# Writing the zeros of the slots' buffer from the first stage on, and pairing the scatters of two mixtures with the shared expert's units

## The chip, the cores and the metric

One Trainium2 chip, one core. The metric is the time of one execution in microseconds of the device, the median of several runs. Engines: PE is TensorE (PEld its weight loads), DVE is VectorE, ACT is ScalarE, POOL is GpSimd, SP is SyncE, which here only issues DMAs; a q behind a name is that engine's sequencer.

## The reference

Sixteen sequences of 128 tokens with 256 features go through four layers. Each layer adds `tanh(g) * attention(layernorm(x))` and then `tanh(g) * ffn(layernorm(x))`. The attentions differ (a decaying sum of the context, masked attention, 32 small heads, attention over channels). The ffn of layer 0 is one linear map. Those of layers 1 to 3 are mixtures of 16 experts beside a shared expert:

```python
logits = h @ router_w.T                       # layer 1; layers 2 and 3 have routers of their own
top_vals, top_idx = jax.lax.top_k(softmax(logits), K)        # K = 4, 2, 4 in layers 1, 2, 3
y = einsum('eni,eih->enh', silu(g) * u, w_down)              # each expert: gate, up, down
routed = einsum('enh,ne->nh', y, comb)
shared = silu(h @ sh_gate) * (h @ sh_up) @ sh_down           # the shared expert, on every token
```

## The kernel before

All tokens stay on the chip as 16 blocks of 128 (`x`, normed in `xn_wide` with 8 more columns of marks). The program is a chain of stages, each a `nc.Block()` in which every engine has its own list of instructions: `setup_and_decay` (attention of layer 0), `linear` (ffn of layer 0), `masked_attention` (layer 1), `mixture(1)`, `many_heads` (attention of layer 2), `mixture(2)`, `channel_heads`, `mixture(3)`, `combine_last`. At the end of a block all five engines meet at a barrier; some stages are followed by a second one (L2566, L2549), where semaphores are freed. A DMA that is in flight needn't have landed at a barrier, but the instruction that issues it has to be over.

A mixture works in two parts. In the first, TensorE, ScalarE and VectorE run the shared expert over all tokens in units: for each pair of blocks, `pieces` units (6 in layer 1, so 48 units; 2 in layer 2, so 16 units). A unit is gate and up products (L2147, or L2152 for the narrow last unit of a pair), the gate activation on ScalarE (L2306, semaphore `sh_gated`, one step a unit), the product with up on VectorE (L2432) and the down product (L2166). In layer 1 the pairs 3 to 6 are a loop at run time. Beside it VectorE routes the tokens: it gives each token a slot row for each of its experts (`row_in`; semaphore `placed`). In layer 1 it does so in two groups of 8 blocks.

GpSimd then scatters the tokens to their slots in DRAM: one indirect DMA per block and choice, 128 rows of 1056 bytes, into `slots_in`. In layer 1 these are 16 x 4 = 64 scatters, all in the mixture. In layer 2 they are 32, of which 14 go out in the attention stage and 18 in the mixture, from block 7 on (L2053). In layer 3 36 go out in the attention stage and the rest in the mixture.

In the second part of a mixture the experts' tiles are worked: SP loads tile by tile from `slots_in` (L2076, only when all scatters have landed), TensorE turns it and multiplies, and GpSimd scatters the results to `slots_out` (L2059).

Not every slot of `slots_in` gets a token, so the whole buffer is filled with zeros first. `write_zeros` (L191 to L194) issues on SP's queue one DMA of 2112 KB for each of the 16 experts, whose source is the cleared tile `xs_wide`. Before the change 5 of them are issued in `linear`, 5 in `masked_attention` and 6 in `mixture(1)`. GpSimd waits for all 16 (`zeroed`) before the first scatter of mixture 1.

`masked_attention` also prepares the gate biases of layer 2: SP loads `bias_raw`; GpSimd splits it in three bf16 parts (L571 to L574) and clears `gbias` (L575); SP writes the parts to DRAM (L559) and reads them back as rows (L562). At L2589 (`root`) GpSimd takes roots of variances for the next norm; `root(pool, 8)` and `root(pool, 9)` end its part of `masked_attention`.

Of the kernel before, what the change touches and what calls it, by code (L numbers as in the profile page):

```python
# [27 lines left out]
NE = 16  # L28
# [99 lines left out]
def _build(nc, io, top):  # L128
# [52 lines left out]
    ZEROS = NE  # L181
# [8 lines left out]
    def write_zeros(eng, first, end):  # L190
        of_block = slots_in.rearrange("(t p) d -> p t d", p=P)  # L191
        for e in range(first, end):
            eng.dma_start(of_block[:, e * NB:(e + 1) * NB, :], xs_wide[:, 0:1, :].broadcast_to([P, NB, W])
                          ).then_inc(zeroed, 16)  # L194
# [49 lines left out]
    def setup_and_decay(measure, root, stats_ready, rooted, zeroed):  # L244

        with ExitStack() as st:
# [1 line left out]
            x_in = [sem(f"x_in{i}") for i in range(4)]  # L248
            ctx_in = [sem(f"ctx_in{i}") for i in range(4)]
            (cleared, gates_ready, own, cw_ready, based, beta_added, sums_done, sumT_ready, in_done, inT_ready,  # L250
             s_done, s_copied, spread, summed, g_ready, x_ready, w_ready) = (
                sem(n) for n in ("cleared", "gates", "own", "cw", "based", "beta", "sums", "sumT", "in", "inT",
                                 "s", "sc", "spread", "summed", "g", "x", "w"))
            numbers_i = sb("numbers_i", [P, ROUTED], I32, st)
            lanes_i = sb("lanes_i", [P, 4], I32, st)
            base_i = sb("base_i", [P, NE], I32, st)
# [16 lines left out]
            @block.sync  # L273
            def _(sp):
                for i in range(4):
                    sp.dma_start(x[:, quarter(i)], io["x"][:, quarter(i)]).then_inc(x_in[i], 16)
                for i in range(4):
                    sp.dma_start(ctx[:, quarter(i)], io["ctx"][:, quarter(i)]).then_inc(ctx_in[i], 16)
                sp.dma_start(ctxT[:], io["ctxT"]).then_inc(ctxT_loaded, 16)
                load_experts(sp, 1)  # L280

            @block.scalar
            def _(act):
# [15 lines left out]
            @block.gpsimd  # L299
            def _(pool):  # L300
                nc.gpsimd.memset(ident[:], 0.0).then_inc(cleared, 1)
                nc.gpsimd.memset(ones[:], 1.0).then_inc(cleared, 1)
                nc.gpsimd.memset(neg_half[:], -0.5).then_inc(cleared, 1)
                pool.iota(numbers_i[:], pattern=[[1, ROUTED]], base=0, channel_multiplier=0).then_inc(cleared, 1)
                pool.iota(lanes_i[:], pattern=[[0, 4]], base=1, channel_multiplier=1).then_inc(cleared, 1)
                pool.iota(base_i[:], pattern=[[NB * P, NE]], base=1, channel_multiplier=0).then_inc(cleared, 1)
                pool.iota(token_i[:], pattern=[[4 * P, NB], [1, 4]], base=-int(FAR), channel_multiplier=4
                          ).then_inc(cleared, 1)
                pool.iota(spare_i[:], pattern=[[P, 8]], base=4 * NB * P - int(FAR), channel_multiplier=1
                          ).then_inc(cleared, 1)  # L310
                pool.wait_ge(cleared, 8)
                nc.gpsimd.affine_select(out=ident[:], in_=ident[:], compare_op=ALU.not_equal, fill=1.0, base=0,
                                        pattern=[[-1, P]], channel_multiplier=1).then_inc(cleared, 1)
                nc.gpsimd.memset(xs_wide[:], 0.0)
                nc.gpsimd.tensor_copy(numbers[:], numbers_i[:])
                for i in range(4):
                    nc.gpsimd.tensor_scalar(lanes[:, i:i + 1], lanes_i[:, i:i + 1], TAG * i, None, ALU.add)
                nc.gpsimd.tensor_copy(expert_base[:], base_i[:])
                nc.gpsimd.tensor_copy(token_rows[:], token_i[:])
                nc.gpsimd.tensor_copy(spare_rows[:], spare_i[:])  # L320
                root(pool, 0)
                root(pool, 1)
                pool.wait_ge(own, 9)
                for b in range(NB):
                    pool.wait_ge(based, b + 1)
                    nc.gpsimd.tensor_tensor(x[:, b, :], x[:, b, :], gg[:, 1, :], ALU.add).then_inc(beta_added, 1)
                pool.wait_ge(w_ready, 1)
                for c in range(C):
                    nc.gpsimd.tensor_tensor(w[:, c, :], w[:, c, :], small["l0_scale"], ALU.mult)
                for b in range(NB):  # L330
                    pool.wait_ge(stats_ready, NB + b + 1)
                    nc.gpsimd.tensor_tensor(xn[:, b, :], xn[:, b, :], gg[:, 0, :], ALU.mult).then_inc(g_ready, 1)
                    if b == 8:
                        root(pool, 2)
                for i in (3, 4, 5):
                    root(pool, i)
# [111 lines left out]
    def linear(measure, root, stats_ready, rooted, kept, blocked):  # L448

        with ExitStack() as st:  # L450
# [3 lines left out]
            block = st.enter_context(nc.Block())  # L454
            XT, Y = bank[0:2], bank[2:6]

            @block.sync
            def _(sp):
                write_zeros(sp, 0, 5)

            @block.gpsimd
            def _(pool):
                for b in range(NB):
# [68 lines left out]
    def masked_attention(measure, root, stats_ready, rooted, kept, blocked):  # L532
        carve = carver(1)
        with ExitStack() as st:
# [16 lines left out]
            def there(b):  # L551
                return 0 <= b < NB

            @block.sync
            def _(sp):
                sp.dma_start(bias_raw, io["l2_gub"]).then_inc(b_in, 16)
                for i in range(3):
                    sp.wait_ge(b_parted, i + 1)
                    sp.dma_start(bias_rows[i].rearrange("(p j) -> p j", j=NE * 2), bias_part[i]).then_inc(b_out, 16)  # L559
                sp.wait_ge(b_out, 48)  # L560
                sp.wait_ge(b_parted, 7)
                sp.dma_start(gbias[0:3], bias_rows).then_inc(b_back, 16)  # L562
                write_zeros(sp, 5, 10)
                sp.wait_ge(b_back, 16)

            @block.gpsimd
            def _(pool):
                step = Chain(pool, b_own)
                pool.wait_ge(b_in, 16)
                for i in range(3):  # L570
                    nc.gpsimd.tensor_copy(bias_part[i], bias_raw).then_inc(b_parted, 1)  # L571
                    if i < 2:
                        pool.wait_ge(b_parted, i + 1)
                        step(nc.gpsimd.tensor_tensor(bias_raw, bias_raw, bias_part[i], ALU.subtract))  # L574
                nc.gpsimd.memset(gbias[:], 0.0).then_inc(b_parted, 1)  # L575
                nc.gpsimd.memset(three_ones[:], 0.0).then_inc(b_parted, 1)
                pool.wait_ge(b_parted, 5)
                nc.gpsimd.memset(three_ones[0:3], 1.0).then_inc(b_parted, 1)
                pool.wait_ge(b_parted, 6)
                pool.sem_inc(b_parted, 1)  # L580
                root(pool, 8)
                root(pool, 9)

            @block.tensor
            def _(pe):
# [1350 lines left out]
    def mixture(layer, rt, carve, t0, scattered, late=0):  # L1936
# [11 lines left out]
        with ExitStack() as st:  # L1948
# [44 lines left out]
            of_group = lambda g, at: bank[3][:, at:at + NE * (groups[g][1] - groups[g][0])]  # L1993
            PRE = [of_group(g, 0).rearrange("p (t e) -> p t e", e=NE) for g in range(len(groups))]
            CNT = [of_group(g, D).rearrange("p (e t) -> p e t", e=NE) for g in range(len(groups))]
            ahead = NB // 2
            late_xT = row_space[:, 7 * D:8 * D].rearrange("p (c q) -> p c q", c=C)
            front_x = lambda b: xT[:, b % 2] if b < ahead else late_xT
# [41 lines left out]
            @block.gpsimd  # L2040
            def _(pool):
                if layer < 3:
                    make_before(pool, rt, tri_ready)
                if layer == 1:
                    nc.gpsimd.tensor_copy(xn_wide[:, :, D + 4:D + 8], token_rows[:]).then_inc(marked, 1)
                    pool.wait_ge(marked, 1)
                if layer == 1:
                    pool.wait_ge(zeroed, 16 * ZEROS)
                for t in range(t0 - late // k, NB):
                    if t in [g[0] for g in groups]:  # L2050
                        pool.wait_ge(placed, 2 * [g[0] for g in groups].index(t) + 2)
                    for i in range(k):
                        pool.indirect_dma_start(out=slots_in, in_=xn_wide[:, t, :], in_offset=None,  # L2053
                                                out_offset=bass.IndirectOffsetOnAxis(ap=row_in[:, t, i:i + 1], axis=0)
                                                ).then_inc(scattered, 16)
                for n in range(total):
                    pool.wait_ge(y_copied, n + 3)
                    pool.wait_ge(places, n + 1)
                    pool.indirect_dma_start(out=slots_out, in_=y[:, n % U, :], in_offset=None,  # L2059
                                            out_offset=bass.IndirectOffsetOnAxis(ap=y_rows[:, n % U:n % U + 1], axis=0)  # L2060
                                            ).then_inc(stored[n % U], 16)

            @block.sync
            def _(sp):
                if layer == 1:
                    write_zeros(sp, 10, ZEROS)
                held = sp.alloc_register(f"block{layer}")
                blocks = slots_in.rearrange("(b p) d -> p b d", p=P)

# [606 lines left out]
```

## Time and profile before

| | us |
|---|---|
| median of 3 runs | 1409.24 |
| lowest, highest | 1405.26, 1410.93 |
| profiled execution, its time | 1406.2 |
| its span, first to last instruction | 1404.5 |
| TensorE busy (matmul) | 1105.6, 79% |
| VectorE busy | 753.7, 54% |
| GpSimd busy | 609.9, 43% |
| ScalarE busy | 487.8, 35% |

Times in the rows are microseconds from the span's start. A row of a timeline gives start, duration, engine, line of the kernel, operation, what is written and read, the number of instructions merged in the row, and in square brackets how long the engine stood idle before it and what released it; "issue" means that it waited for nothing that the profile shows. Lines are those of the kernel before. Issue instructions of DMAs on SP are shown with the time that SP spent on them, which isn't the time to landing.

### The profile page before, as it was taken

The numbers are of one execution on the slowest core, as the hardware profiler recorded it, in microseconds if no ns is written. First come the engines' busy times: TensorE is split into PE (matmuls) and PEld (weight loads), VectorE is DVE, ScalarE is ACT, GpSimd is POOL, SyncE is SP. The second block draws the span as 40 slices with busy tenths as digits, with TensorE's granted clock in tenths as the row PEclk, the third lists the DMA queues.
The fourth block names the chain that finished last, engine by engine and source line by source line (L and its number), as shares of the span: only waits on it lengthen the run. The fifth ranks groups of instructions, "written<-read, shape, count | busy, mean of one in ns | idle before, by whom it ended". The sixth has DMA issues, their size and how long they took to land. (4 is left out here: it accounts for less than half of the span.)

```text
span 1404.5 us, 25581 instructions
## 1 busy us (share of the span) xinstructions
PE 1105.6 (79%) x7222; PEld 815.2 (58%) x7223; DVE 753.7 (54%) x2787; ACT 487.8 (35%) x1309; POOL 609.9 (43%) x961
## 2 busy tenths in 40 slices
PE   4476984399999996799997779958887756599980
PEld 4364863287777774466665567845554434478770
DVE  6857432013444444687862555557777554365557
ACT  0054210011333332266653124424764422144440
POOL 5552056600333334565552404545564554345560
PEclk9998896699999998699996999977998876899995
DMA  9598942200333333211500114540002311256547
GB/s 407 160 309 266 340 142 89 92 0 16 104 106 106 106 106 107 77 47 61 219 25 32 66 43 134 155 157 2 2 2 117 137 67 66 85 136 165 145 132 299
DMA packets 92302, 169.45 MB, mean 121 GB/s; under 512 B 11103, under 2 KB 70751, under 8 KB 91231
## 3 DMA queue, kind: packets, MB, share of 16 engines
q1 hardware_dynamic: 72825, 114.71, 26.2%
q0 software_dynamic: 17664, 48.91, 9.6%
q10 hardware_dynamic: 1728, 4.79, 0.9%
q8 instruction: 44, 0.72, 0.2%
q14 instruction: 41, 0.33, 0.1%
HBM read 82.75 MB, written 85.61 MB: 120 GB/s over the span
## 5 line engine op out<-in xcount | busy, mean ns | idle before, releaser
L2236 PE MATMUL bank<-weights,xT 128*128 x832 | 241.0, 412 | 0.8 <-ACT xT L2330 0.7
L2059 POOL DMA_INDIRECT slots_out<-weights,y_rows x128 | 123.2, 962 | 155.3 <-DVE y_rows L2501 81.8
L2059 POOL DMA_INDIRECT slots_out<-pack,y_rows x80 | 77.0, 962 | 199.4 <-DVE y_rows L2501 190.8
L2053 POOL DMA_INDIRECT slots_in<-xn_wide,row_in x110 | 106.4, 968 | 124.1 <-DMA slots_in<-xs_wide 50.2
L2236 PEld LDWEIGHTS bank<-weights,xT 128*128 128x128 f32 x832 | 142.4, 191 | 25.9 <-issue 2.2
L2147 PE MATMUL bank<-xT,weights 128*128 128x256 f32 x416 | 113.0, 420 | 20.3 <-ACT xT L2294 16.7
L2330 ACT COPY xT<-bank 128x256 f32<-128x256 f32 x208 | 77.5, 373 | 111.3 <-PE bank L2228 104.2
L1471 PE MATMUL bank<-ctx,weights 32*128 32x256 f32 x512 | 80.5, 461 | 37.5 <-DVE weights L1627 27.9
L2147 PEld LDWEIGHTS bank<-xT,weights 128*128 128x128 f32 x416 | 85.7, 211 | 40.1 <-ACT xT L2294 14.1
L2432 DVE TENSOR_TENSOR rows<-rows,bank 128x256 f32<-128x256 f32 (+1 forms) x56 | 22.5, 402 | 147.4 <-ACT rows L2306 105.7
L1544 ACT ACTIVATE weights<-bank 128x512 f32<-128x512 f32 x128 | 72.6, 597 | 79.0 <-PE bank L1479 60.7
L1627 DVE TENSOR_REDUCE weights<-bank 128x2 f32<-128x512 f32 x128 | 86.0, 682 | 21.1 <-PE bank L1471 16.2
L2166 PE MATMUL bank<-weights,rows 128*128 128x256 f32 x256 | 73.4, 404 | 28.1 <-issue 21.8
L2478 DVE TENSOR_TENSOR weights<-weights,bank 128x128 f32<-128x128 f32 x128 | 36.9, 288 | 92.8 <-ACT weights L2334 83.9
L2306 ACT ACTIVATE rows<-bank 128x256 f32<-128x256 f32 (+1 forms) x56 | 20.7, 370 | 185.7 <-PE bank L2147 97.1
L1471 PEld LDWEIGHTS bank<-ctx,weights 32*128 32x128 f32 x512 | 51.5, 216 | 54.2 <-issue 24.4
L2253 PE MATMUL bank<-weights,pack 88*128 x320 | 82.2, 379 | 0.0
L1479 PE MATMUL bank<-weights 32*128 32x256 f32 x512 | 78.9, 451 | 1.4 <-ACT weights L1544 1.4
L2253 PE MATMUL bank<-weights 128*128 x256 | 77.3, 385 | 0.8 <-ACT weights L2338 0.8
L2478 DVE TENSOR_TENSOR pack<-pack,bank 128x176 f32<-128x176 f32 x80 | 27.1, 338 | 92.5 <-ACT pack L2334 78.7
L971 ACT ACTIVATE weights<-bank 128x512 f32<-128x512 f32 x128 | 71.5, 605 | 12.2 <-PE bank L865 11.8
L2166 PEld LDWEIGHTS bank<-weights,rows 128*128 128x128 f32 x256 | 48.7, 201 | 42.4 <-issue 33.3
(432 smaller groups left out, 2479.7 us busy)
## 6 DMA issues: line engine op xcount, KB each, us to landing
slots_in<-xs_wide SPq DMA_DIRECT2D x16, 2112.0 KB, 18.9
weights<-slots_in SPq DMA_DIRECT2D x96, 132.0 KB
xs_wide<-slots_in SPq DMA_DIRECT2D x72, 132.0 KB
weights<-slots_out SPq DMA_DIRECT2D x17, 512.0 KB, 17.4
rows<-slots_out SPq DMA_DIRECT2D x16, 512.0 KB, 3.3
weights<-in_l_gu SPq DMA_DIRECT2D x1, 7040.0 KB
pack<-slots_in SPq DMA_DIRECT2D x40, 132.0 KB
weights<-in_l_gu SPq DMA_DIRECT2D x1, 4608.0 KB, 16.2
```

The costliest lines, as they stand in the source:

```text
L971: nc.scalar.activation(e[:, G * c + g].rearrange("p j q -> p (j q)"), S[g][:], ACT.Exp, scale=HD ** -0.5).then_inc(e_ready, 1)
L1471: last = nc.tensor.matmul(score_bank(N * bs + ns)[:, j * L:(j + 1) * L], xh[bs % 2][rows, j, qh * P:(qh + 1) * P], ctx[rows, bs, :], start ...
L1479: last = nc.tensor.matmul(key_bank(N * b + n)[:, j * L:(j + 1) * L], km[b % 2][rows, j, c * P:(c + 1) * P], xm[b % 2][rows, j, :], start=T ...
L1544: nc.scalar.activation(eT[:, n].rearrange("p j q -> p (j q)"), key_bank(t)[:], ACT.Exp, scale=HD ** -0.5).then_inc(e_ready, 1)
L1627: nc.vector.tensor_reduce(peak[b % 2][:, qh, at:at + step_j + 1:step_j], score_bank(s)[:].rearrange("p (j l) -> p j l", j=2), AX.X, ALU.ma ...
L2053: pool.indirect_dma_start(out=slots_in, in_=xn_wide[:, t, :], in_offset=None, out_offset=bass.IndirectOffsetOnAxis(ap=row_in[:, t, i:i + 1 ...
L2059: pool.indirect_dma_start(out=slots_out, in_=y[:, n % U, :], in_offset=None, out_offset=bass.IndirectOffsetOnAxis(ap=y_rows[:, n % U:n % U ...
L2147: last = nc.tensor.matmul(out[:, side * D:(side + 1) * D], shared_gu[:, c, at:at + P], xp[:, c, :], start=(c == 0), stop=(c == C - 1))
L2166: last = nc.tensor.matmul(s_Y[t % 2][:, 0:D], sh_h4[:, n % ring, u * P:(u + 1) * P], shared_dn[:, i, :], start=(i == 0), stop=(i == pieces ...
L2236: last = nc.tensor.matmul(out, xT[:, n.c % 2, c, :], flat(gu_w[:, ds(e, 1), c, :]), start=(c == 0), stop=(c == C - 1 and layer != 2))
L2253: last = nc.tensor.matmul(Y[n.c % 2][:, 0:D], hT[:, n.c % 2, i, :], flat(dn_w[:, ds(e, 1), i, :]), start=(i == 0), stop=(i == parts - 1))
L2330: nc.scalar.copy(flat(xT[:, n.c % 2]), XT[n.c % 2][:, 0:D]).then_inc(xT_ready, 1)
```

## The change

- `write_zeros` for all 16 experts stands at the end of SP's list in `setup_and_decay`, behind all loads and behind a new semaphore `blank`, which GpSimd raises when it has cleared `xs_wide`. The calls in `linear`, `masked_attention` and `mixture(1)` go.
- The four small DMAs for the gate biases in `masked_attention` are issued by GpSimd instead of SP, in the same order. GpSimd waits for the three stores before `root(pool, 8)`, and for the read back at its end.
- In mixtures 1 and 2 GpSimd waits before every second scatter for one more `sh_gated`: pair m for gate 10 + m in layer 1 (gates 10 to 41 of 48), for 6 + m in layer 2 (6 to 14 of 16). Layer 3 is unchanged.

```diff
             @block.sync                      # setup_and_decay
                 load_experts(sp, 1)
+                sp.wait_ge(blank, 1)
+                write_zeros(sp, 0, ZEROS)
...
-                nc.gpsimd.memset(xs_wide[:], 0.0)
+                nc.gpsimd.memset(xs_wide[:], 0.0).then_inc(blank, 1)
...
-            @block.sync                      # linear
-            def _(sp):
-                write_zeros(sp, 0, 5)
...
-            @block.sync                      # masked_attention
-            def _(sp):
-                sp.dma_start(bias_raw, io["l2_gub"]).then_inc(b_in, 16)
-                for i in range(3):
-                    sp.wait_ge(b_parted, i + 1)
-                    sp.dma_start(bias_rows[i].rearrange("(p j) -> p j", j=NE * 2), bias_part[i]).then_inc(b_out, 16)
-                sp.wait_ge(b_out, 48)
-                sp.wait_ge(b_parted, 7)
-                sp.dma_start(gbias[0:3], bias_rows).then_inc(b_back, 16)
-                write_zeros(sp, 5, 10)
-                sp.wait_ge(b_back, 16)
             @block.gpsimd
                 step = Chain(pool, b_own)
+                pool.dma_start(bias_raw, io["l2_gub"]).then_inc(b_in, 16)
                 pool.wait_ge(b_in, 16)
...
-                pool.sem_inc(b_parted, 1)
+                for i in range(3):
+                    pool.dma_start(bias_rows[i].rearrange("(p j) -> p j", j=NE * 2), bias_part[i]).then_inc(b_out, 16)
+                pool.wait_ge(b_out, 48)
+                pool.dma_start(gbias[0:3], bias_rows).then_inc(b_back, 16)
                 root(pool, 8)
                 root(pool, 9)
+                pool.wait_ge(b_back, 16)
...
+            send_from = {1: 10, 2: 6, 3: 0}[layer]          # mixture
...
                     for i in range(k):
+                        if layer < 3 and i % 2 == 0:
+                            pool.wait_ge(sh_gated, send_from + ((t - t0) * k + i) // 2)
                         pool.indirect_dma_start(out=slots_in, in_=xn_wide[:, t, :], in_offset=None,
...
             @block.sync                      # mixture
-                if layer == 1:
-                    write_zeros(sp, 10, ZEROS)
```

## Rows read from the trace of the kernel before

**Rows 1.** List of waits, whole span: who for whom, us in total, times, longest

```profile
POOL slots_in L2053 <- DMA slots_in<-xs_wide: 50.2, 1, 50.2
```

**Rows 2.** Timeline of GpSimd: attention stage, mixture 1, tiles of mixture 2

```profile
119.61 1.64 POOL L2589 TENSOR_TENSOR rstd<-var,neg_half 128x8 f32<-128x8 f32 x1 [7.66 <-DVE var L2583]
...
132.28 0.20 POOL L2591 TENSOR_TENSOR offset<-nmean,rstd 128x8 f32<-128x8 f32 x1
136.35 0.21 POOL L1931 MEMSET pack<- 128x128 f32 x1 [3.87 <-POOLq L2566]
...
187.38 1.24 POOL L2053 DMA_INDIRECT slots_in<-xn_wide,row_in  x1 [50.23 <-DMA slots_in<-xs_wide]
...
226.93 0.96 POOL L2053 DMA_INDIRECT slots_in<-xn_wide,row_in  x1 [0.30 <-issue]
234.19 0.96 POOL L2053 DMA_INDIRECT slots_in<-xn_wide,row_in  x1 [6.30 <-DVE xn_wide L1869]
...
273.56 0.96 POOL L2053 DMA_INDIRECT slots_in<-xn_wide,row_in  x1 [0.31 <-issue]
...
902.03 0.96 POOL L2059 DMA_INDIRECT slots_out<-weights,y_rows  x1 [0.77 <-issue]
```

**Rows 3.** Timeline of TensorE in mixture 1: first and last of each slow stretch

```profile
202.40 0.44 PE L2152 MATMUL bank<-xT,weights 128*64 128x128 f32 x4
...
230.74 0.59 PE L2166 MATMUL bank<-weights,rows 128*128 128x256 f32 x1 [1.51 <-issue]
...
252.07 0.27 PE L2152 MATMUL bank<-xT,weights 128*64 128x128 f32 x1 [0.45 <-issue]
...
278.06 0.59 PE L2166 MATMUL bank<-weights,rows 128*128 128x256 f32 x1 [2.21 <-issue]
```

**Rows 4.** Timeline of ScalarE in mixture 1: gates of units 12, 30 and 48

```profile
187.99 0.28 ACT L2306 ACTIVATE rows<-bank 128x128 f32<-128x128 f32 x1
...
298.46 0.28 ACT L2306 ACTIVATE rows<-bank 128x128 f32<-128x128 f32 x1
...
344.46 0.28 ACT L2306 ACTIVATE rows<-bank 128x128 f32<-128x128 f32 x1 [1.51 <-PE bank L2152]
```

**Rows 5.** Timeline of TensorE in mixture 2

```profile
811.40 3.78 PE L2147 MATMUL bank<-rows,weights 128*128 128x256 f32 x8 [7.93 <-ACT rows L2294]
```

**Rows 6.** DMAs of zeros: ns to issue (min/median/max), and us to landing

```profile
L193 SPq DMA_DIRECT2D slots_in<-xs_wide x16: 389/6212/6849, 72.1 to 166.6; - x16
...
DMA to landing us min/median/max: 7.9/18.9/19.9
```

**Rows 7.** The page's DMA issues: count, KB each, median us to landing

```profile
slots_in<-xs_wide SPq DMA_DIRECT2D x16, 2112.0 KB, 18.9
```

**Rows 8.** Timeline of SP: the last loads' issue, and the zeros' issues merged

```profile
9.49 1.38 SPq L215 DMA_DIRECT2D weights<-in_l_sdn  x1
72.07 21.73 SPq L193 DMA_DIRECT2D slots_in<-xs_wide  x5
...
112.37 60.77 SPq L193 DMA_DIRECT2D slots_in<-xs_wide  x11
```

**Rows 9.** Waits of SP's queue at barriers after stage one, linear, attention (two)

```profile
SPq L246 <- PEq L246: 61.0, 1, 61.0
...
SPq L450 <- PEq L450: 3.5, 1, 3.5
...
SPq L2566 <- PEq L2566: 0.7, 1, 0.7
...
SPq L534 <- PEq L534: 0.2, 1, 0.2
```

**Rows 10.** Windows: length, busy of PE, PEld, DVE, ACT, POOL, clock, DMA share, GB/s

```profile
50.00:60.00 10.00, 1.82 (x5) 0.91 (x3) 9.90 (x28) 0.00 (x0) 8.33 (x11) 1.00 0.69 159
...
62.00:64.00 2.00, 0.00 (x0) 0.00 (x0) 1.90 (x11) 0.00 (x0) 0.51 (x1) 1.00 0.26 104
...
140.00:173.00 33.00, 31.02 (x168) 27.25 (x167) 15.09 (x76) 8.97 (x23) 0.00 (x0) 0.80 1.09 340
```

**Rows 11.** The page's DMA queues: packets, MB, share of 16 engines

```profile
q8 instruction: 44, 0.72, 0.2%
```

More of the change, by code:

```diff
@@ L250, in setup_and_decay @@
             (cleared, gates_ready, own, cw_ready, based, beta_added, sums_done, sumT_ready, in_done, inT_ready,
-             s_done, s_copied, spread, summed, g_ready, x_ready, w_ready) = (
+             s_done, s_copied, spread, summed, g_ready, x_ready, w_ready, blank) = (
                 sem(n) for n in ("cleared", "gates", "own", "cw", "based", "beta", "sums", "sumT", "in", "inT",
-                                 "s", "sc", "spread", "summed", "g", "x", "w"))
+                                 "s", "sc", "spread", "summed", "g", "x", "w", "blank"))
             numbers_i = sb("numbers_i", [P, ROUTED], I32, st)
```

## The prediction

> **What bounds the kernel now.** I read the list of waits first, then the timelines of SP, GpSimd, TensorE and ScalarE in the first 345 us, and last the DMA windows. The waits point to GpSimd: its first scatter of mixture 1 stands 50.2 us waiting for the zeros [rows 1]. That wait by itself costs little. Mixture 1 begins at 136.35 [rows 2], TensorE and ScalarE work on the shared expert meanwhile, and nothing there needs the scatters yet. The price comes after. Scatters run back to back from 187.38 to 227.9 and from 234.19 to 274.5, one every 1.27 us (0.96 busy, 0.30 between) [rows 2]. From 202.40 TensorE starts single matmuls "issue"-idle between them until 230.74, and again from 252.07 until 278.06 [rows 3]. It waits for no engine's data there; it is slow in starting its own instructions. Both times it comes back 3 to 5 us after the last scatter of the run.
>
> Size of that stall: the gate activations of the shared expert stand at 298.46 and at 344.46 with 18 units between, so an undisturbed unit takes 46.0 / 18 = 2.56 us. From 187.99 (12th gate) to 344.46 (48th) there are 36 units: 92 us undisturbed, 156.5 us in the trace [rows 4]. **64 us are lost to the scatters.** In mixture 2 one stall of the same look costs 7.9 us [rows 5].
>
> The other thing to see is SP. Its issue of a 2112 KB DMA of zeros takes 6.2 us in the median and 0.4 at the least, and such a DMA lands up to 19.9 us after its issue [rows 6, 7]: SP gets about two of them ahead of the DMA engines, then stands until one has landed. Five hold it 21.7 us, eleven 60.8 us [rows 8]. And the end of each stage is a barrier that SP joins. At the end of the attention stage SP waited 0.2 us at the first barrier (L534) and 0.7 at the second (L2566) [rows 9], so it came last; GpSimd was done at 132.48 and began again at 136.35 after 3.87 us idle [rows 2]. The five zeros of that stage held up all engines for 3.87 - 0.9 - 0.2, say 2.8 us.
>
> **The change, part by part.**
>
> *Zeros from stage one.* All 16 now stand behind the loads on SP's queue, in a stage that ends at 72 us and in which SP today waits 61.0 us for the others at the barrier [rows 9]. SP has issued its loads at 10.9 us [rows 8]. The DMA engines are busy with the loads to about 64 us: share 0.69 in 50 to 60, still 0.26 in 62 to 64 [rows 10]. Some engines are done earlier, but each DMA of zeros is spread over them, and its landing waits for the slowest. Zeros move at 340 GB/s with the engines full (share 1.09) [rows 10]: 2112 KB is 2.163 MB, 6.35 us each, 16 make 101.6 us. If the slowest engine starts at 62, the last lands at 163; if all work had been packed evenly, at about 156. Today the last issue ends at 112.37 + 60.77 = 173.1 and the zeros are there at 187.4 at the latest, 14 us later [rows 2, 8]. So SP leaves stage one at 163 - 13 = 150; bounds 143 and 156. The other engines are done at 72.0 and stand. **Cost +78 us** (+71 to +84). Nothing hides it: no work of another stage can pass the barrier.
>
> *What this takes away.* The 2.8 us at the end of the attention stage go. In the linear stage SP reached its barrier 3.5 us early [rows 9], so the five zeros that leave it were covered: 0. The eleven later issues lay beside mixture 1's work: 0.
>
> *Bias rows by GpSimd.* Four small DMAs move from SP's queue to GpSimd's. GpSimd idles 7.66 us before its root at 119.61 [rows 2], and the zeros have landed before this stage begins, so transfers meet empty engines. Four issues at the 0.96 us of its scatters are 4 us, plus landings of a few us. Only the last root (ready at 132.48) is on the path. Cost 0; upper bound 8 us, should each of the three waits take 5 us and only the idle time absorb them; below nothing it can't go, since SP did the same in a hidden place.
>
> *Scatters of mixture 1 in pairs.* Before each pair GpSimd waits for one more gate, from the 10th to the 41st. Queued behind this wait are only more scatters; who waits for them is SP (all 64) before it loads tiles. The 41st gate is 7 units or 18 us before the 48th, so the loads aren't late. The 64 scatters start where they start today, at the 10th gate instead of 187.38 in today's time, and need 32 units instead of two runs of 41 us.
>
> Does this keep TensorE going? A pair costs GpSimd 2 x (0.96 + 0.30) = 2.52 us, and an undisturbed unit is 2.56 us. So the pairs leave almost no pause; the rate is that of today's runs. What the wait does give is feedback: if TensorE stalls, no gate comes, the scatters stop after the present pair, and TensorE recovers after 3 to 5 us. Today's stalls begin 15 and 18 us after a run begins [rows 2, 3]. 32 units are 82 us, so about five stalls, each 4.4 us (recovery, with part of the pair before it): 22 us come back. **Gain 64 - 22 = 42 us.** Bounds: 64, if pairs never stall it (in mixture 2's tiles one scatter every 1.7 us goes on without such idle time [rows 2]); and about 5, if every loop turn and every instruction block of each engine stalls 6 to 8 us. I take the middle, for the density is nearest to that of today's runs.
>
> The Trainium skill ("Runtime: NRT & Kernel Launch", Instruction fetch mechanics) says that each engine's instructions come in 16 KiB blocks over a DMA queue of its own, and that a taken branch can force such a fetch. The page's instruction queue shows 44 packets and 0.72 MB, 16 KB each [rows 11], which agrees. By that rule stalls would fall where an engine needs its next block while scatters are going, more often in the loop of pairs 3 to 6, and the gain would be nearer 30 than 64.
>
> *Scatters of mixture 2.* 18 in nine pairs, behind gates 6 to 14 of 16. Today's stall is 7.9 us [rows 5]; one short one may remain: **gain 4 us** (0 to 8). The last pair leaves two units, some 5 us, for landing and loads, which just do.
>
> **Sum.** +78 - 2.8 - 42 - 4 = +29 us on the profiled execution (1406.2 us, span 1404.5): 1435 us. The median of the runs shown, 1409.24, is 3 us above it; I say **1437 us**.
>
> **Rivals.**
> 1. *Held at stage one, stalls partly back* (above): 1420 to 1462. Chance 0.50.
> 2. *Held, but pairs remove all stalls.* +78 - 2.8 - 64 - 8 = +3: about 1412, 1404 to 1420. For it: steady scatters in the tiles disturb nobody. Against: 2.52 of 2.56 us is no pause. Chance 0.26. With it the kernel is unchanged as measured.
> 3. *SP isn't held in stage one*, because the queue takes more DMAs than seen or zeros overtake the tail of the loads. Then SP leaves below 72 us and the sum is -2.8 - 42 - 4 = -49, about 1360, down to 1335 with all stalls gone. It decides from the point where SP's last issue ends before 72 us. Against it: the loads do go out without a hold, in 10.9 us, but the third DMA of zeros already waits for the first one to land [rows 6, 7, 8]. Chance 0.09.
> 4. *Pairs don't help*: every unit with scatters is slow. With a gain of 5 in all the sum is +70: 1480. For it: same density and now twice as many units under scatters. Against it: the feedback. Chance 0.15.
>
> Beside rival 3, the Trainium skill ("DMA: Bandwidth & Descriptors", Issuing engines are not separate DMA queues) says that DMAs of all issuing engines share the same 16 engines and that issuing costs the sequencer little. By this rule SP would be away early and the time would be rival 3's; the trace's 6.2 us issue is against it.
>
> **How the numbers follow.** 0.5% is 7 us, about what a measurement can tell from no change. Faster (below 1402): rival 3 and a sliver of 2, 0.11. Same (to 1416): most of rival 2 and little of 1, 0.19. Slower: the rest, 0.70. Range: 1404 to 1472, which leaves out rival 3 and half of rival 4, about 0.2; the likeliest case's own is 1420 to 1462.
>
> **What the new profile would show.** SP's zeros follow its loads without a gap, its last issue ends near 150; all other engines idle from 72 to about 150, released by the barrier; the linear stage starts there. If it starts at 72, rival 3 holds. The attention stage lasts 36 us instead of 38.8. In mixture 1 scatters stand in pairs behind ScalarE's gates, the 12th to 48th gate take about 114 us (92: rival 2; above 145: rival 4), and TensorE's "issue" idle falls into short pieces of 3 to 5 us. Mixture 2's shared expert is 4 us shorter. Everything behind is shifted and otherwise as before. The prediction is wrong first of all if the hold in stage one is not 71 to 84 us; next if the pairs' stalls are not about a third of today's.

## The result and the profile after

The changed kernel takes 1433.59 us (median of 4, 1429.44 to 1437.66), the kernel before in the same comparison 1410.09 (4, 1405.26 to 1414.42): ratio 1.0167, 95% interval 1.0123 to 1.0212. It is slower by 1.7%. The forecast was 1437 us, and "slower" had a chance of 0.70. The profiled execution took 1429.44 us with a span of 1427.6, 23.1 more than before.

The timeline of SP in the changed kernel (start, duration; 16 issues in one row), and its list of waits from 60 to 220 us:

```profile
11.09 142.02 SPq L193 DMA_DIRECT2D slots_in<-xs_wide  x16
```

```profile
ACT xn_wide L495 <- PEq L246: 115.6, 1, 115.6
...
DVE kept L512 <- PEq L246: 83.4, 1, 83.4
```

SP stands in its issues from 11.09 to 153.1, and the others stand at the barrier of stage one (L246). The windows show how completely (columns: busy us of PE, PEld, DVE, ACT and POOL with instructions, granted clock, DMA share, GB/s):

```profile
0.00:72.00 72.00, 33.15 (x112) 27.02 (x113) 51.68 (x158) 2.95 (x7) 39.27 (x68) 1.00 0.93 326
72.00:153.00 81.00, 0.00 (x0) 0.00 (x0) 0.00 (x0) 0.00 (x0) 0.19 (x1) 1.00 1.08 342
```

For 81 us no engine works and the DMA engines write zeros at 342 GB/s, the rate of [rows 10]. ScalarE began the linear stage at 72.08 before and begins it at 153.53 now, 81.5 us later.

The timeline of GpSimd, changed kernel: the bias rows' read back, the start of mixture 1, its first and last scatter. They answer to [rows 2]:

```profile
189.79 0.57 POOL L570 DMA_DIRECT2D gbias<-bias_rows  x1 [1.42 <-DMA bias_rows<-pack]
...
214.36 0.21 POOL L1922 MEMSET pack<- 128x128 f32 x1 [1.54 <-POOLq L2558]
...
262.77 1.13 POOL L2047 DMA_INDIRECT slots_in<-xn_wide,row_in  x1 [47.62 <-ACT rows L2298]
...
359.76 0.96 POOL L2047 DMA_INDIRECT slots_in<-xn_wide,row_in  x1 [0.30 <-issue]
```

Mixture 1 starts 78.0 us later than before (136.35). By the first rows of ScalarE in each stage the attention stage takes 36.2 us instead of 38.8, so it gave back 2.6, and the linear stage 24.6 instead of 25.5. GpSimd waits for a gate now, not for zeros. The gates of units 12 and 48, timeline of ScalarE, against [rows 4]:

```profile
266.80 0.28 ACT L2298 ACTIVATE rows<-bank 128x128 f32<-128x128 f32 x1
...
381.14 0.28 ACT L2298 ACTIVATE rows<-bank 128x128 f32<-128x128 f32 x1 [1.51 <-PE bank L2144]
```

114.3 us instead of 156.5: 42 came back. But the stalls that remain look different from those of before. From the timeline of the changed kernel, all engines, 281 to 288 us:

```profile
281.61 0.38 ACT L2298 ACTIVATE rows<-bank 128x256 f32<-128x256 f32 x1 [2.21 <-PE bank L2139]
...
282.37 1.09 PE L2144 MATMUL bank<-xT,weights 128*64 128x128 f32 x16
...
284.00 0.96 POOL L2047 DMA_INDIRECT slots_in<-xn_wide,row_in  x1 [0.30 <-issue]
286.68 0.59 ACT L2286 COPY xT<-bank 128x512 f32<-128x512 f32 x1 [4.68 <-remote]
...
287.72 0.96 POOL L2047 DMA_INDIRECT slots_in<-xn_wide,row_in  x1 [2.75 <-ACT rows L2298]
```

The products of the narrow unit are over at 283.46, TensorE goes on without a pause, and ScalarE's copy, which waits for them, starts 3.2 us later, with no releaser of this kernel ("remote"). Then TensorE and GpSimd both wait for ScalarE. This comes about once in each pair of blocks. From 262 to 385 us the matmuls have only 1.0 us of "issue" idle left.

The shift over time: 81.5 at the start of the linear stage, 78.0 at the start of mixture 1, 36.7 at its end, 35.8 at the first pair of mixture 2, 26.5 at the start of `channel_heads`, 23.1 at the end.

### The profile page after: what moved, and what is told of

Read it like the earlier page. It is cut to its first block and busy times, and to the rows that moved or that the text cites. A ratio compares the mean times of both kernels' runs of the same rounds, so it can differ in the third digit from the quotient of the medians.

```text
span 1427.6 us, 25582 instructions
## 1 busy us (share of the span) xinstructions
PE 1093.3 (77%) x7222; PEld 807.5 (57%) x7223; DVE 754.1 (53%) x2787; ACT 487.8 (34%) x1309; POOL 613.1 (43%) x966
## 5 line engine op out<-in xcount | busy, mean ns | idle before, releaser
L2139 PEld LDWEIGHTS bank<-xT,weights 128*128 128x128 f32 x416 | 86.2, 213 | 45.2 <-issue 23.6
L1618 DVE TENSOR_REDUCE weights<-bank 128x2 f32<-128x512 f32 x128 | 86.0, 682 | 19.5 <-PE bank L1462 16.1
L477 PE MATMUL bank<-ident,xn_wide 128*128 128x128 f32 x32 | 6.7, 300 | 102.2 <-ACT xn_wide L495 102.2
L2158 PE MATMUL bank<-weights,rows 128*128 128x256 f32 x256 | 69.6, 394 | 7.6 <-DVE x L2432 6.2
```

What stands on the lines that cost most here:

```text
L1618: nc.vector.tensor_reduce(peak[b % 2][:, qh, at:at + step_j + 1:step_j], score_bank(s)[:].rearrange("p (j l) -> p j l", j=2), AX.X, ALU.ma ...
L2139: last = nc.tensor.matmul(out[:, side * D:(side + 1) * D], shared_gu[:, c, at:at + P], xp[:, c, :], start=(c == 0), stop=(c == C - 1))
L2158: last = nc.tensor.matmul(s_Y[t % 2][:, 0:D], sh_h4[:, n % ring, u * P:(u + 1) * P], shared_dn[:, i, :], start=(i == 0), stop=(i == pieces ...
```

## Experiments: the two halves apart

Theory: the zeros cost about 80 us because SP is held at the barrier of stage one, and the pairs gain some 50 by themselves. Rival: the halves are tied together (fewer zeros in flight make the stall smaller, not the pairs). Four kernels, on one chip, on which the kernel before took 1406.10. Whether the 1433.59 of the changed kernel come from the same chip isn't known.

**Pairs alone** is the kernel before plus

```diff
+            send_from = {1: 10, 2: 6, 3: 0}[layer]
...
+                        if layer < 3 and i % 2 == 0:
+                            pool.wait_ge(sh_gated, send_from + ((t - t0) * k + i) // 2)
```

> The kernel before with the waits of the pairs alone; zeros and bias rows stay where they were. Theory (the two halves of the change add up): the linear stage starts at 72, the 12th to the 48th gate take about 114 us as in the changed kernel instead of 156, mixture 2's gates are 13 us shorter and its tiles lose 3: 1410 - 42 - 13 + 3 = 1358 us (1350 to 1370). The scatters still start at 187.4, when the last zeros are there. Rival (the stalls became smaller because the zeros had left the DMA engines, not because of the pairs): 12th to 48th gate stay above 145 us, and the time is 1395 to 1410.

Measured: 1355.01 us (1347.03 to 1361.49), ratio 0.9609 (0.953 to 0.9688). 12th to 48th gate 110.1 us.

**Zeros alone** is the changed kernel without those waits.

> The changed kernel without the waits of the pairs: all 16 DMAs of zeros from stage one, bias rows by GpSimd, scatters back to back. Theory: linear stage starts at 153, 81 us late, 3 come back at the end of the attention stage, and the scatters cost TensorE the same 64 us as before: 1410 + 81 - 3 = 1488 us (1480 to 1495). Rival (the zeros were part of that stall): 12th to 48th gate come down to about 114 us without pairs, and the time is about 1433 to 1446.

Measured: 1484.33 us (1482.24 to 1489.85), ratio 1.0541 (1.0468 to 1.0613); 12th to 48th gate 150.4 us. Both expected times held, and the halves add up: the pairs are worth 51.1 us without the zeros' move (1406.1 - 1355.0) and 50.7 with it (1484.3 - 1433.6), nearer to each other than the spread of the runs (8 to 14 us) can tell. The rival falls.

This kernel also shows what comes late. TensorE, VectorE and ScalarE in the timeline of zeros alone, while 32 scatters run from 260.06 to 300.31:

```profile
285.41 0.73 PE L2137 MATMUL bank<-xT,weights 128*128 128x256 f32 x1 [1.03 <-issue]
306.24 0.77 PE L2172 MATMUL bank<-pack 128*128 128x128 f32 x2 [20.11 <-issue]
```

```profile
305.86 0.22 DVE L1812 TENSOR_SCALAR pack<-pack 128x128 f32<-128x128 f32 x1
```

```profile
291.72 0.38 ACT L2296 ACTIVATE rows<-bank 128x256 f32<-128x256 f32 x1 [18.10 <-issue]
305.11 0.66 ACT L2296 ACTIVATE rows<-bank 128x256 f32<-128x256 f32 x2 [13.01 <-remote]
```

The product that the gate of 291.72 takes was over at 277.27 by TensorE's rows, and those of the two gates at 305.11 by 286.2. TensorE's own 20.11 us are a consequence, though the row says "issue": in the kernel its next instruction (L2172) waits for VectorE's choice of experts (L1812), and VectorE's list has that behind its product with the gate of 305.11. What TensorE loses directly is smaller: single matmuls that start 0.8 and 1.03 us late, like those of [rows 3], in the middle of a unit, where the kernel has no wait. ScalarE comes back 4.8 us after the last scatter of the run.

The kernel before has the same. The timeline of its ScalarE:

```profile
218.82 0.38 ACT L2306 ACTIVATE rows<-bank 128x256 f32<-128x256 f32 x1 [19.46 <-remote]
232.90 0.38 ACT L2306 ACTIVATE rows<-bank 128x256 f32<-128x256 f32 x1 [13.70 <-remote]
```

By the rows the product for the first of them was over at 199.02. But the trace also records the updates of semaphores, which these views don't list: TensorE's update for this product stands at 218.80, 19.8 us after that, and ScalarE starts 0.02 us after the update. In the changed kernel the copy of 286.68 has its update at 286.60, for products over at 283.46. ScalarE's and VectorE's own updates come at once in the same place (199.37 for a gate that ends at 199.36, 199.82 for a product that ends at 199.81). So ScalarE isn't slow to start: **late is TensorE's signal to it, or the true end of TensorE's product**, since the ends of matmuls are modelled. "remote" says just this, that an update came with no instruction ending beside it. The first late one in the kernel before is that of the gate of 198.97, whose product was over at 195.77, 8 us after the first scatter.

**Eight zeros first**: only the count in stage one changes, the other 8 go out in mixture 1.

```diff
-                write_zeros(sp, 0, ZEROS)
+                write_zeros(sp, 0, 8)
...
+                if layer == 1:
+                    write_zeros(sp, 8, ZEROS)
```

> The changed kernel, but only 8 DMAs of zeros from stage one and 8 from mixture 1. Theory: what holds SP is the count of DMAs, 6.24 us each: it leaves stage one at 153.1 - 8 x 6.24 = 103.2, 31 us late. The eight in mixture 1 take 50 us and land by about 180, before the 10th gate. 1434 - 50 = 1384 us (1377 to 1392). Rival (SP waits for the landing of the loads, or for all of its DMAs at the barrier): stage one ends above 115 and the time is above 1396.

Measured: 1378.64 us (1368.06 to 1383.91), ratio 0.977 (0.9686 to 0.9853). ScalarE begins the linear stage at 102.73: 30.7 us late, 31 were expected. So the cost follows the count: 8 DMAs more cost 81.5 - 30.7 = 50.8 us, 6.35 each, the time in which the DMA engines move one.

**Zeros dealt out**, 3, 4, 5 and 4 by stage:

```diff
-                write_zeros(sp, 0, ZEROS)
+                write_zeros(sp, 0, 3)
...
+            @block.sync
+            def _(sp):
+                write_zeros(sp, 3, 7)
...
+            @block.sync
+            def _(sp):
+                write_zeros(sp, 7, 12)
...
+                if layer == 1:
+                    write_zeros(sp, 12, ZEROS)
```

> Pairs and bias rows by GpSimd as in the changed kernel, with the zeros dealt out so that they fit into each stage: 3 from stage one (the third issue ends at 153.1 - 13 x 6.24 = 72.0), 4 in the linear stage (25 us of 25), 5 in the attention stage (31 of 36) and 4 in mixture 1. Theory: no stage ends late, the attention stage is 3 us shorter, scatters begin with the 10th gate: 1434 - 81 = 1353 us (1346 to 1360), below the kernel with pairs alone by 3 to 6 us. Rival: the third issue of stage one or the fourth of the linear stage ends late by one DMA, and each such miss gives 6 us back: 1358 to 1366.

Measured: 1349.48 us (1335.0 to 1351.62), ratio 0.9545 (0.9459 to 0.9632). The linear stage starts at 72.56 (72.20 with pairs alone) and mixture 1 at 134.39 (136.48): no stage is held, 2 us are gained there. The difference to pairs alone, 5.5 us, is within the spread of the two.

## Experiments: what is it in the scatters

My theory was feedback: at the density of before, starving (matmuls and signals of TensorE that come late for no cause in the program) begins after some 15 us, and the wait for a gate lets the engines recover. The rivals were the density itself, the loop, and the bytes. Four kernels with one profiled execution each, on a second chip, on which the kernel before took 1409.62.

**Paced**: the kernel before, no waits on gates, but a small piece of work between two scatters of mixture 1.

```diff
+    pace_space = sb("pace_space", [P, 128])
...
+                        if layer == 1:
+                            nc.gpsimd.memset(pace_space[:], 0.0).then_inc(paced, 1)
+                            pool.wait_ge(paced, t * k + i + 1)
```

> The kernel before with no waits on gates: GpSimd only clears 128x128 elements after each scatter of mixture 1 and waits for that, which makes one scatter every 1.6 us or so instead of 1.27. In the changed kernel the 64 stand 1.54 us apart on average (262.77 to 359.76). Theory (feedback: the scatters must stop when a gate is late): pacing alone doesn't stop the starving, 12th to 48th gate stay above 135 us (before 156.5). Rival (rate: density alone decides): 12th to 48th gate come to 105 to 120 us as with the pairs.

Measured: 1345.54 us, 12th to 48th gate 96.8 us. The timeline of GpSimd in it, and the windows (columns as above):

```profile
200.05 0.96 POOL L2055 DMA_INDIRECT slots_in<-xn_wide,row_in  x1 [0.28 <-issue]
201.02 0.22 POOL L2059 MEMSET pace_space<- 128x128 f32 x1
201.51 0.96 POOL L2055 DMA_INDIRECT slots_in<-xn_wide,row_in  x1 [0.28 <-issue]
```

```profile
200.00:227.00 27.00, 25.79 (x141) 21.09 (x140) 9.95 (x40) 5.61 (x14) 21.93 (x37) 1.00 0.26 95
```

One scatter every 1.46 us instead of 1.27, for all of the 92 us, and TensorE is busy 25.8 of 27 us; in the same stretch of before it was 8.4, at a clock of 0.64 instead of 1.00. The same stretch of before:

```profile
200.00:227.00 27.00, 8.43 (x30) 4.72 (x29) 2.98 (x16) 0.38 (x1) 20.29 (x23) 0.64 0.29 105
```

Nothing stopped the scatters when an engine was late, so feedback isn't needed: **my theory fell, and spacing the scatters is enough, with a steep step between 1.27 and 1.46 us**. The 96.8 us lie even below the rival's 105 to 120. One thing isn't told apart: between two scatters stand both 0.2 us of work and a wait for it, so GpSimd can't have the next scatter queued. That the interval decides, and not this wait, is argued, not shown. For it speak the pairs: their waits are often over already when GpSimd comes to them, and then starts are late again. Their mean interval is 1.54 us, but a backlog goes out in runs of up to ten at 1.27, and the late starts come in or right behind such runs (the row of 284.00 above is the last of eight).

**One scatter a gate** halves the density up to the 48th gate; 26 come behind it (the expectation says 25).

```diff
-                        if layer < 3 and i % 2 == 0:
+                        if layer == 1:
+                            pool.wait_ge(sh_gated, min(48, 10 + t * k + i))
+                        elif layer == 2 and i % 2 == 0:
```

> Pairs kernel, but in mixture 1 one scatter behind each gate from the 10th on, and the last 25 after the 48th gate. Half the density in the stretch of the gates. Theory (what is left of the stall, some 3 to 4 us in each pair of blocks, comes from scatters near the moment at which ScalarE needs something): 36 units take 92 to 98 us, each pair of blocks 15.5 to 16.5 us instead of 17 to 20.8. Rival (what is left is a fixed price of the waits or of the loop, not of the scatters): 105 us or more. The end of the kernel is later by some 30 us, since the remaining scatters stand bare.

Measured: 1369.13 us; 12th to 48th gate 93.4 us, the pairs of blocks 15.3 to 16.1 us each. The expectation held: that is within 1.4 us of the 92 of an undisturbed stretch, so 64 us was the right size for the loss of before. The list of ScalarE's waits from 188 to 282 us in this kernel, and from 188 to 300 us with pairs alone:

```profile
ACT rows L2311 <- PE bank L2152: 66.0, 30, 2.9
ACT xT L2299 <- PE bank L2157: 8.9, 6, 1.6
ACT rows L2311 <- PE bank L2157: 1.6, 1, 1.6
```

```profile
ACT rows L2309 <- PE bank L2150: 57.1, 24, 5.6
ACT xT L2297 <- remote: 20.1, 5, 5.2
ACT rows L2309 <- issue: 10.3, 4, 4.0
ACT rows L2309 <- remote: 3.5, 1, 3.5
```

"remote" is the mark of the starving, TensorE's late signals. In this stretch of mixture 1 it comes to 69.2 us in the kernel before, 23.6 with pairs alone, none with one scatter a gate and none when paced. Later in those kernels, where scatters go out unpaced, it is there again (22 us in the gates of mixture 3 when paced).

**Unrolled**: pairs alone, with `looped = range(0)`, so the middle pairs of blocks are written out.

> Pairs kernel with the four middle pairs of blocks of mixture 1's shared expert written out in place of the loop, so no engine takes a branch there. Theory (stall at the branch: each turn of the loop makes an engine fetch instructions, which wait behind the scatters): the late copies of ScalarE, once in each pair of blocks, go away in pairs 4 to 7; 12th to 48th gate 92 to 100 us instead of 110. Rival (the fetches come with the number of instructions, or it is no fetch at all): the late starts stay, 12th to 48th gate 107 to 115 us, perhaps at other places.

Measured: 1349.49 us, 12th to 48th gate 109.5 us (110.1 with the loop), "remote" 24.1 us. The late starts come without any branch. The prediction weighed the Trainium skill's rule ("Runtime: NRT & Kernel Launch", Instruction fetch mechanics) that a taken branch can force a fetch: these stalls don't come from that. Nor do they come from fetches without a branch. The list of DMA queues of the kernel before, from 200 to 330 us, in which nearly all of its stall lies (queue, kind: packets, MB, share of 16 engines; the second line is the next one of the list):

```profile
q0 software_dynamic: 2640, 7.44, 15.7%
issues: line engine op xcount, KB each, median us to landing
```

Only the scatters' queue moved anything; no packet of an instruction queue did. (The page has two of these over the whole kernel: that of [rows 11] and q14, with 41 packets of 8 KB, which the prediction left out.)

**Few bytes**: as many scatters with as many rows, but 24 of 264 columns, into a tensor that nobody reads; the real scatters follow behind the 48th gate.

```diff
+                        if layer == 1:
+                            pool.indirect_dma_start(out=io["narrow_slots"], in_=xn_wide[:, t, 0:24], in_offset=None,
+                                                    out_offset=bass.IndirectOffsetOnAxis(ap=row_in[:, t, i:i + 1],
+                                                                                         axis=0)).then_inc(narrow, 16)
+                            continue
```

> The kernel before, but its 64 scatters of mixture 1 write only 24 of 264 columns, to a tensor that nobody reads; the real ones follow behind the 48th gate and a wait for the narrow ones stands behind them. So in the stretch of the gates there are as many scatters with as many descriptors, and a tenth of the bytes. Theory (count of descriptors and their issue, not bytes): 12th to 48th gate 140 to 160 us as before. Rival (bytes on the DMA engines or in memory): 92 to 110 us. The end comes some 60 to 80 us late in any case; only the stretch is read.

Measured: 1494.33 us. Gates 12 and 48 in the timeline of ScalarE, and TensorE between them:

```profile
191.04 0.28 ACT L2320 ACTIVATE rows<-bank 128x128 f32<-128x128 f32 x1
...
344.50 0.28 ACT L2320 ACTIVATE rows<-bank 128x128 f32<-128x128 f32 x1 [1.51 <-PE bank L2166]
```

```profile
226.53 0.37 PE L2166 MATMUL bank<-xT,weights 128*64 128x128 f32 x1 [1.73 <-issue]
230.03 0.37 PE L2166 MATMUL bank<-xT,weights 128*64 128x128 f32 x1 [3.12 <-issue]
232.13 0.37 PE L2166 MATMUL bank<-xT,weights 128*64 128x128 f32 x1 [1.73 <-issue]
```

153.5 us, as with full rows, while the DMA engines move 10 GB/s instead of 105. Bytes are not the cause; the number of scatters or of their rows in a given time is. (The packets aren't quite as many as expected: 32 a scatter instead of 48 by the DMA lists.) A scatter takes GpSimd 966 ns with 24 columns and 962 with 264. The Trainium skill ("Perfetto Trace Analysis", DMA Instruction — SWDGE (GPSIMD)) says that the profile's end of such an instruction is the end of its writing of descriptors, not of the transfer; a time that doesn't depend on the bytes agrees.

## Experiments: the best of both, on another chip

The last four ran on a third chip. **On it the kernel before took 1274.06 us (23 executions, 22 of them from 1272.3 to 1279.3, one 1486.44), not 1406 to 1410.** That was not foreseen, and it changes what these four can say.

**Paced, dealt out** has the zeros of 3, 4, 5 and 4, no waits on gates, and the pace in mixtures 1 and 2 (`if layer < 3:`).

> Zeros 3, 4, 5 and 4 by stage and bias rows by GpSimd, no waits on gates; instead a clearing of 128x128 elements after each scatter of mixtures 1 and 2. The kernel before with the pace in mixture 1 alone took 1345.5. Theory: 3 us less at the end of the attention stage, and mixture 2's stall of 12.7 goes too: 1345 - 3 - 12 = 1330 us (1322 to 1336), 19 below the kernel with the same zeros and pairs. Rival (pace instead of pairs doesn't help 18 scatters in a short stage): 1340 to 1345.

Measured: 1272.88 us (median of 12), ratio 0.9985 (0.9972 to 0.9997). Neither range holds it, since both start from 1345 us of another chip; the pace gained nothing here.

**Paced in all mixtures** drops that condition.

> The same with the pace in mixture 3 as well. In the kernel before TensorE stood 10.2 us for ScalarE's late copy at 1213 while 28 scatters of mixture 3 ran from 1172.9 to 1210.6. Theory: some 8 of these come back, against 28 x 0.2 = 6 us by which the scatters end later, of which nothing is exposed: 1322 us (1316 to 1328). Rival (the loads wait for the later scatters): the gain is eaten, 1327 to 1334, as without it.

Measured: 1278.47 us (median of 12), ratio 1.0031 (1.0017 to 1.0045), and 5.6 us slower than the one above, which is 28 x 0.2.

**Short pace** is paced with 4 elements cleared instead of 128 (one scatter every 1.36 us).

> As the paced kernel, but GpSimd clears only 4 elements in each partition between two scatters, so one comes every 1.35 to 1.42 us instead of 1.46 (1.27 in the kernel before). Looks for the point at which the starving begins. Theory (a rate above which a store of pending work fills: the steeper the excess, the sooner): between the two, 12th to 48th gate 97 to 130 us. If it's 97 the point lies below this rate, if it's above 140 it lies close to 1.46.

**Half the rows** is few bytes with `xn_wide[0:64, t, 0:24]` and 64 indices.

> As the kernel with scatters of 24 columns (the real ones follow behind the 48th gate), but each of the 64 now writes only the rows of 64 partitions instead of 128, back to back. Theory (too many descriptors in a given time): if GpSimd's time for one scatter stays near 0.96 us, the descriptors in a given time are half as many and the 12th to the 48th gate take 92 to 100 us instead of 156; if it halves too, they stay dense and the stretch is longer than 100. Rival (the instructions of GpSimd themselves disturb the others): 140 us or more though descriptors are half as many.

Measured: 1272.85 and 1362.58 us; 12th to 48th gate 93.3 and 93.0 us. A scatter of 64 rows takes GpSimd 0.90 us, one every 1.20. Neither kernel says anything on its question, for this chip shows no starving at all: in the lists of waits of its four traces "remote" isn't found once in the whole span. The kernel before has its 64 scatters unpaced there too and takes 1274 us; no trace of it was taken there. And see mixtures 2 and 3 of short pace, whose scatters go out at 1.27 us without a pace: from the start of mixture 2's weights' load to its first tile's load 126.5 us pass (609.1 to 735.6), on the second chip in the paced kernel, whose mixture 2 is the same, 147.7 (614.1 to 761.8); from the load of mixture 3's weights (989.5 and 1015.4) to the first tile 107.3 against 142.1. The two kernels differ there in nothing. Of the 72.7 us between their profiled executions, 4.6 lie ahead of `many_heads`, 21.5 between its start and mixture 2's first tile, 34.6 between that and mixture 3's, the rest behind. Short pace is thus inconclusive on the point at which starving begins, and half the rows on descriptors against instructions.

What the pace costs where nothing starves, in the timeline of TensorE at the first tile of mixture 3, without and with pace there:

```profile
1097.82 0.66 PE L2232 MATMUL bank<-ident,xs_wide 128*128 128x128 f32 x2 [5.82 <-DMA xs_wide<-slots_in]
```

```profile
1103.93 1.45 PE L2233 MATMUL bank<-ident,xs_wide 128*128 128x128 f32 x4 [11.29 <-DMA xs_wide<-slots_in]
```

SP may load tiles only when all scatters have landed. TensorE waits 5.5 us longer; nothing covers the 28 late scatters. This was the rival of that expectation, in a sharper form: there was no stall to win back either.

## Why the prediction was right, point by point

The two large terms and their mechanisms are right; that the time came within 4 us of 1437 is in part luck. On the profiled execution the forecast was +29 us and +23.1 were measured: the hold is 3.5 us longer than forecast, while mixture 2 and what stands behind it gave back 8.7 more.

- **Hold in stage one, +78.** Measured +81.5 (72.08 to 153.53), inside 71 to 84. The mechanism is shown: by the 81 us in which nothing runs, and by the dose (8 DMAs instead of 16: 30.7). It was sized 3 us short: the last issue ended at 153.1, not 150.
- **Attention stage, -2.8.** Measured -2.6. The linear stage, put at 0, is 0.8 us shorter; it takes 24.6 to 25.6 us in the six traces of the kernel before, the changed one and the first four experiments, with no order that the zeros would explain.
- **Bias rows, 0.** Right: GpSimd waits 1.6 us for the load and 1.42 for the stores, and the last root isn't later than its data.
- **Pairs in mixture 1, -42.** Measured -42.1, 114.3 us for the 36 units as forecast. The size of the loss, 64 us, is shown by one scatter a gate (93.4 us). The way to the number was only half right, so that it fits to 0.1 us is luck: "if TensorE stalls, no gate comes, the scatters stop after the present pair, and TensorE recovers" happens, but what comes late is mostly TensorE's signal to ScalarE, seven times and not five, and what I denied to the pairs, pauses between scatters, works without any feedback. That "the rate is that of today's runs" holds for the runs inside the pairs, not for their mean (1.54 us). Of the stall before, too, the prediction saw only TensorE's late matmuls, not the signals, which come late from 8 us after the first scatter on (it has 15 and 18 us).
- **Pairs in mixture 2, -4.** Mis-sized. The stretch of gates fell from 61.2 to 48.5 us, -12.7, since the wait of 7.9 us in [rows 5] was one of two delays of that stall; its tiles then took 3.4 us longer, so 9.3 are left. With pairs alone mixture 2 is 12.4 us shorter (155.2 instead of 167.7), and without pairs it stays as it was (167.2 in zeros alone).
- **Behind it** 3.4 us more came back between the start of `channel_heads` and the end, which the prediction didn't have. Of these 2.3 lie in `channel_heads`, a stage that takes 235.0 to 241.0 us in the same six traces. The cause is open.
- **Rival 3** (SP isn't held), and the rule of the Trainium skill beside it ("DMA: Bandwidth & Descriptors", Issuing engines are not separate DMA queues; issuing costs the sequencer little), fell with the 142.02 us of SP's row: these issues cost 6.2 us each once about two are outstanding.
- **Rival 2** fell on these chips, by 22 us of late starts. On the third chip there would be nothing to win back, and the change would leave its 81 us bare. That wasn't run.

What stays open: why TensorE's signals and its single matmuls come late. It is no instruction that a DMA queue brings, since none came in 130 us, and for the single matmuls it is no semaphore of the kernel, since none stands between them. Whether TensorE's work really ends so late or only its signal does, no view shows. Open too are why one of the three chips of the experiments doesn't starve, whether the interval or the wait in the pace is the cure, and where between 1.27 and 1.46 us the step lies.

## What to carry to other kernels

Fit DMAs that hold their engine (here 2048 rows of 1056 bytes, 6.2 us each) to the stage that issues them: ask where the issuing engine will be when the others reach the barrier, and deal them out (here 3, 4, 5 and 4 took 1349 us, 16 at once 1434). When engines start late without a cause in the profile, look for a run of scatters, and try 0.2 us of other work between two of them before tying them to another engine's progress. And time such a cure on more than one chip: what was worth 64 us on one was worth nothing on another, and cost 5.6 us where the scatters stood bare.

## What the runs showed of the hardware that was not expected

- While scatters of 128 rows run back to back (one every 1.27 us), single matmuls start up to 3.2 us late, and TensorE's semaphore update reached ScalarE 19.8 us after the end of the product by TensorE's rows, in the kernel before; with one every 1.46 us, with a clearing and a wait for it between, neither is seen. The bytes don't matter (10 or 105 GB/s), nor does a loop (109.5 and 110.1 us), and no instructions came over a DMA queue while it lasted.
- It depends on the chip: the same kernel takes 1406 and 1410 us on two and 1274 on a third, whose four traces hold no "remote" wait.
- TensorE's clock goes with it: a mean of 0.64 of full speed from 200 to 227 us of before, where it is busy for 8.4 of 27 us, and 1.00 in the paced kernel, where it is busy for 25.8. So 0.64 is part of the time at 2.4 GHz and part at 1.2.
